# First layer of a two-layer block: half of the second GroupNorm's sums as running arrays instead of Gram products

## The reference

```
x = x + linear_attention(group_norm(x))     # layer 0
x = x + gated_conv(group_norm(x))           # layer 1
```

## Time and profile before

| what | value |
|---|---|
| three runs | 6730.23, 6728.38, 6723.05 us |
| median | 6728.38 us |
| the profiled execution's own time | 6717.27 us |
| its span | 6715.5 us |
| mean granted TensorE clock, share of full speed | 0.96 |
| busy over the span: PE, PEld, DVE, ACT, POOL | 85%, 78%, 67%, 54%, 61% |

### The profile page before, as it was taken

One profiled execution on the slowest core, in us unless ns is written; L12 is line 12 of the kernel. 1 busy time (PEld: TensorE's weight loads), 2 busy tenths in 40 slices (PEclk: granted clock), 3 DMA queues, 4 the chain that ended last, 5 costly groups with the idle time before them and its releaser, 6 DMA issues. The chain is left out here.

```text
span 6715.5 us, 144257 instructions
## 1 busy us (share of the span) xinstructions
PE 5725.9 (85%) x51796; PEld 5234.1 (78%) x51796; DVE 4511.4 (67%) x5284; ACT 3640.0 (54%) x4872; POOL 4125.6 (61%) x3608
## 2 busy tenths in 40 slices
PE   5789999999999999999984368888888888888887
PEld 5678888888888888888874368777877878777787
DVE  6367777777777777777763786666666666666653
ACT  5555555555555555555540445555555555555554
POOL 0146666666666666666667677676676767676751
PEclk8899999999999999999997789999999999999999
DMA  5356676666766667666656469899999999999987
GB/s 130 123 157 205 205 216 202 206 198 207 212 209 199 200 206 211 207 198 207 190 168 184 122 176 262 252 261 249 259 261 253 265 255 262 245 256 251 258 247 212
DMA packets 1239334, 1441.35 MB, mean 215 GB/s; under 512 B 142960, under 2 KB 1025396, under 8 KB 1238516
## 3 DMA queue, kind: packets, MB, share of 16 engines
q1 hardware_dynamic: 1238516, 1431.07, 75.0%
HBM read 999.09 MB, written 431.64 MB: 213 GB/s over the span
## 5 line engine op out<-in xcount | busy, mean ns | idle before, releaser
L1257 PE MATMUL psC<-wide,xhl 128*128 128x256 bf16 x6144 | 1037.1, 279 | 37.1 <-DVE xhl L1455 15.2
L1187 POOL TENSOR_TENSOR stage<-stage,nrow 128x1024 f32<-128x1024 f32 x240 | 620.0, 2583 | 407.8 <-DMA stage<-x_by_block_row 397.0
L1254 PE MATMUL psC<-wide,xhl 128*128 128x192 bf16 x6144 | 863.3, 250 | 0.0
L1204 POOL COPY down<-xhl 48x448 f32<-48x448 f32 x512 | 533.2, 1041 | 520.9 <-PE psC L1263 421.9
L813 POOL TENSOR_TENSOR y<-y,grow 128x1024 f32<-128x1024 f32 x256 | 603.9, 2359 | 323.7 <-DVE y L657 323.7
L1455 DVE SCALAR_TENSOR_TENSOR xhl<-xhl,psC 128x512 f32<-128x512 f32 x512 | 348.8, 682 | 503.7 <-ACT xhl L1348 503.0
L824 POOL TENSOR_TENSOR q<-q,qinv 128x1024 f32<-128x1024 f32 x256 | 490.0, 1914 | 308.6 <-DVE qinv L731 308.6
L1263 PE MATMUL psC<-narrow,down 128*128 128x96 bf16 x6144 | 527.3, 210 | 171.5 <-DMA narrow<-toeplitz_narrow 98.1
L657 DVE TENSOR_TENSOR y<-psProj,rstd 128x1024 f32<-128x1024 f32 x256 | 313.5, 1225 | 516.0 <-POOL rstd L805 516.0
L1348 ACT ACTIVATE xhl<-psC 128x512 f32<-128x512 f32 x512 | 304.3, 599 | 636.7 <-PE psC L1263 635.1
L1254 PEld LDWEIGHTS psC<-wide,xhl 128*128 128x128 bf16 x6144 | 639.3, 115 | 12.2
(11 more groups left out here) (181 smaller groups left out, 14276.2 us busy)
## 6 DMA issues: line engine op xcount, KB each, us to landing
wide<-toeplitz_wide SPq DMA_DIRECT2D x1024, 140.0 KB, 4.5
xa<-in_x SPq DMA_DIRECT2D x256, 512.0 KB, 4.7
xb<-in_x SPq DMA_DIRECT2D x256, 512.0 KB, 3.8
xc<-in_x SPq DMA_DIRECT2D x256, 512.0 KB, 5.7
x_rows<-xc SPq DMA_DIRECT2D x256, 512.0 KB
res<-x_rows SPq DMA_DIRECT2D x256, 512.0 KB, 7.2
out<-res SPq DMA_DIRECT2D x256, 512.0 KB, 6.4
stage<-x_by_block_row SPq DMA_DIRECT2D x225, 512.0 KB, 7.2
```

The source lines that it names most:

```text
L1187: nc.gpsimd.tensor_tensor(v, v, nrow[:, 0:1, :].to_broadcast([P, NP_, C]), ALU.mult).then_inc(s_scaled, 1)
L1204: nc.gpsimd.tensor_copy(dst[lo, :, :, 0:last], src[lo, :, 0:NQ, CW:])
L1254: nc.tensor.matmul(dst[:, :, :, 2:], lhs, tab[:, :, 32 + part * 12:44 + part * 12], start=False, stop=False)
L1257: nc.tensor.matmul(dst, lhs, tab[:, :, part * 16:part * 16 + 16], start=(n == 0), stop=False)
```

## The change

The chunk's 8 rows are parted. The Gram product takes rows 0 to 3 (TG = 4), so 8 passes of TensorE where there were 16. The other four rows (TS = 4), a [128, 4, 128] slice, go this way: GpSimd adds them to `acc1` at the end of the step in which it made x1; ScalarE squares them into `sq` at the beginning of the next step, ahead of qT; VectorE adds `sq` to `acc2` right behind y. At n = 2 of the next image TensorE's `turn_sums`, behind the projection, multiplies the four rows of `acc1` and of `acc2` by a column of ones and so adds over the partitions: into column 128 of psG and into a column of its own. `take_gram` moves from behind y to the end of VectorE's step, waits for that, and has one addition more. SyncE waits for the square and the running sum too before it reloads xc.

```diff
--- before.py
+++ after.py
@@ -255,6 +255,8 @@
     CHUNKS = IMGS * NCH
     W1 = C + 1
     BK = 96
+    TG = 4
+    TS = TPC - TG
     STORES = [16 * n for n in (4, 7, 4, 7)]
     with ExitStack() as ctx:
         sb = lambda n, s, d=F32: ctx.enter_context(nc.sbuf_tensor(n, s, d))
@@ -308,6 +310,9 @@
         norm_old = sb("norm_old", [P, 2])
         gram = sb("gram", [P, C])
         gsum = sb("gsum", [P, 2])
+        sq = sb("x1_squared", [P, TS, C])
+        acc1 = sb("x1_sum", [P, TS, C])
+        acc2 = sb("x1_square_sum", [P, TS, C])
         psR = [ps(f"psR{k}", [P, CT]) for k in range(2)]
         psO = ps("psProj", [P, CT])
         psC = ps("psCtx", [P, 512])
@@ -363,6 +368,11 @@
         g_done = sem("b_gram")
         s_gram = sem("b_gram_masked")
         g_taken = sem("b_gram_taken")
+        s_sq = sem("b_squared")
+        s_acc1 = sem("b_sum_added")
+        s_acc2 = sem("b_square_added")
+        s_fin = sem("b_sums_turned")
+        s_accgo = sem("b_sum_begun")
         block = ctx.enter_context(nc.Block())
         NCONST = 5
 
@@ -414,6 +424,8 @@
                         if not isinstance(img, int) or gc + 1 >= 4:
                             sp.wait_ge(s_store[k], img * (STORES[k] * NCH // 4) + (n + 1) // 4 * STORES[k])
                         sp.wait_ge(g_done, upto(gc - 2))
+                        sp.wait_ge(s_acc1, upto(gc - 2))
+                        sp.wait_ge(s_sq, upto(gc - 2))
                         sp.dma_start(xc[k][:, :, 0:C], x_chunk(img + (n + 1) // NCH, (n + 1) % NCH)
                                      ).then_inc(s_xc[k], 16)
                     if live(img, gc - 2):
@@ -465,10 +477,20 @@
                 if m == 0:
                     pe.wait_ge(g_taken, img)
                 v = xc[m % 4]
-                for t in range(TPC):
+                for t in range(TG):
                     mm = nc.tensor.matmul(psG[:, 0:W1], v[:, t, 0:C], v[:, t, :],
-                                          start=(m == 0 and t == 0), stop=(m == NCH - 1 and t == TPC - 1))
+                                          start=(m == 0 and t == 0), stop=False)
                 mm.then_inc(g_done, 1)
+
+            def turn_sums(img):
+                pe.wait_ge(s_acc1, img * NCH)
+                pe.wait_ge(s_acc2, img * NCH)
+                one = xc[0][:, 0, C:W1]
+                for t in range(TS):
+                    nc.tensor.matmul(psG[:, C:W1], acc1[:, t, :], one, start=False, stop=(t == TS - 1))
+                for t in range(TS):
+                    mm = nc.tensor.matmul(psG[:, W1:W1 + 1], acc2[:, t, :], one, start=(t == 0), stop=(t == TS - 1))
+                mm.then_inc(s_fin, 1)
 
             def turn_ek(n, ga, gb):
                 pe.wait_ge(k_exped, gb)
@@ -574,6 +596,8 @@
                         nc.tensor.transpose(psC[:, 128:256], accn[:], ident[:]).then_inc(s_m, 1)
                     if live(img, gc - 1):
                         project(img, n, gc)
+                    if n == 2 and image_live(img - 1):
+                        turn_sums(img)
                     if n == 0 and image_live(img):
                         pe.wait_ge(s_m, img * 7 + 4)
                         nc.tensor.matmul(psC[:, 256:384], wqkv[:, 2 * C:3 * C], ctxg[:], start=True, stop=True
@@ -588,6 +612,10 @@
             def image(img, steps):
                 for n in range(steps):
                     ga, gb, gc = indices(img, n)
+                    if live(img, gc - 3):
+                        act.wait_ge(s_x1, gc - 2)
+                        act.wait_ge(s_acc2, upto(gc - 3))
+                        nc.scalar.activation(sq[:], xc[(n - 3) % 4][:, TG:, 0:C], ACT.Square).then_inc(s_sq, 1)
                     if live(img, gb - 2):
                         act.wait_ge(qt_ready, gb - 1)
                         act.wait_ge(o_ready, upto(gc - 1))
@@ -740,13 +768,25 @@
                 mx = qmax[:, n % 2, :].unsqueeze(2).to_broadcast([P, TPC * HEADS, DH])
                 nc.vector.tensor_tensor(qv, v, mx, ALU.subtract).then_inc(q_subbed, 1)
 
+            def add_squares(img, n, gc):
+                dve.wait_ge(s_sq, gc - 2)
+                if (n - 3) % NCH == 0:
+                    if image_live(img - 1):
+                        dve.wait_ge(s_fin, img)
+                    nc.vector.tensor_copy(acc2[:], sq[:]).then_inc(s_acc2, 1)
+                else:
+                    dve.wait_ge(s_acc2, gc - 3)
+                    nc.vector.tensor_tensor(acc2[:], acc2[:], sq[:], ALU.add).then_inc(s_acc2, 1)
+
             def take_gram(img, gc):
-                dve.wait_ge(g_done, gc - 2)
+                dve.wait_ge(s_fin, img)
                 nc.vector.tensor_copy(gsum[:, 0:1], psG[:, C:W1])
                 nc.vector.tensor_tensor(gram[:], psG[:, 0:C], ident[:], ALU.mult).then_inc(s_gram, 1)
-                dve.wait_ge(s_gram, img * 2 - 1)
+                dve.wait_ge(s_gram, img * 3 - 2)
                 nc.vector.tensor_reduce(gsum[:, 1:2], gram[:], AX.X, ALU.add).then_inc(s_gram, 1)
-                dve.wait_ge(s_gram, img * 2)
+                dve.wait_ge(s_gram, img * 3 - 1)
+                nc.vector.tensor_tensor(gsum[:, 1:2], gsum[:, 1:2], psG[:, W1:W1 + 1], ALU.add).then_inc(s_gram, 1)
+                dve.wait_ge(s_gram, img * 3)
                 at = slice(img - 1, img) if isinstance(img, int) else bass.ds(img - 1, 1)
                 nc.vector.tensor_copy(sums2[:, :, at].squeeze(2), gsum[:]).then_inc(g_taken, 1)
 
@@ -768,8 +808,8 @@
                         dve.wait_ge(s_m, img * 7 + 7)
                         dve.wait_ge(o_ready, img * NCH)
                         nc.vector.tensor_tensor(M[:], psC[:, 384:512], brow[:], ALU.add).then_inc(s_mready, 1)
-                    if n == 2 and image_live(img - 1):
-                        take_gram(img, gc)
+                    if live(img, gc - 3):
+                        add_squares(img, n, gc)
                     if n == 0 and image_live(img + 1):
                         norm_weights(img, gb)
                     if n == 0 and live(img, gb - 1):
@@ -785,6 +825,8 @@
                             add_up(n, gb)
                     if live(img, gb):
                         centre_q(n, gb)
+                    if n == 2 and image_live(img - 1):
+                        take_gram(img, gc)
 
             all_images(dve, image)
 
@@ -822,6 +864,18 @@
                         qv = q[k][:].rearrange("p t (h d) -> p (t h) d", d=DH)
                         iv = qinv[:, k, :].unsqueeze(2).to_broadcast([P, TPC * HEADS, DH])
                         nc.gpsimd.tensor_tensor(qv, qv, iv, ALU.mult).then_inc(s_qn, 1)
+                    if live(img, gc - 2):
+                        v = xc[(n - 2) % 4][:, TG:, 0:C]
+                        pool.wait_ge(s_x1, gc - 1)
+                        if (n - 2) % NCH == 0:
+                            if image_live(img - 1):
+                                pool.wait_ge(s_fin, img)
+                            if not isinstance(img, int):
+                                pool.sem_inc(s_accgo, 1)
+                            nc.gpsimd.tensor_copy(acc1[:], v).then_inc(s_acc1, 1)
+                        else:
+                            pool.wait_ge(s_acc1, upto(gc - 2))
+                            nc.gpsimd.tensor_tensor(acc1[:], acc1[:], v, ALU.add).then_inc(s_acc1, 1)
 
             all_images(pool, image)
```

## The result

| what | before | after |
|---|---|---|
| median of four runs each | 6729.31 us | 6788.15 us |
| lowest and highest run | 6723.05, 6737.33 | 6767.97, 6791.86 |
| ratio after/before | | 1.0081, 95% from 1.0058 to 1.0103 |
| the profiled execution's own time, its span | 6717.27, 6715.5 | 6767.97, 6764.5 |
| end of layer 0 in it | 3659.51 | 3697.09 |

The change costs 59 us. The forecast said +70 (6798, range 6742 to 6865). Of the 49 us between the two profiled spans 37.6 arise in layer 0 and 11.4 behind it.

A forecast was written before the change was run, and what follows sets the result against it. The bound was a closed two-step loop through the Gram product, 12.19 us a step. Full images 44, last but one 3, last 21, tail 1: together 69 on 6728, rounded 6798 us; range 6742 to 6865.

The forecast's parts named there:

- two-step loop through the Gram product: Closed loop across engines in full steps, today's bound: 24.42 us over two steps, falling to 23.91, 11.96 a step.
- ScalarE loop: One-step loop from projection through ScalarE's work and `keys` to the next projection: 11.80 us, plus 0.50 for the square, 12.30.
- port loop: One-step loop from y through centring and row sums to the next y: 11.94 us, plus 0.38, 12.32.
- The lock's delay: VectorE's addition behind y holds back GpSimd's multiplication by g: 0.54 less some 0.16 of overlapping start-up, taken as 0.38 us.
- full-block rival: GpSimd's multiplication by g delayed by all of 0.54: port loop 12.48, 28 us more, 6826; chance 0.18.
- n = 1 to 4 [...] +0.9 net, the weakest figure: Steps n = 1 to 4 of each full image: gains and losses net +0.9 us, bounds -1 to +3.
- the step n = 0 [...] +0.85: Step n = 0 of each full image: 0.6 for the addition before the statistics, VectorE ending some 0.25 later; +0.85 us, an estimate.
- The last image: GpSimd is the bound there: running sum 1.1 and lock 0.38 add 1.5 us on each of 14 steps, 21 us.
- the clock should not answer: TensorE's granted clock stays despite the halved Gram: in the prologue it is busy 8.80 of 10.82 us and granted 1.00.
- Lock lost: GpSimd takes the port before the addition every step: 13.9 us a step, +1.7 on 165 steps, about 7030; chance 0.06.
- Loops shorter than added up: The square fits in ScalarE's slack, leaving 11.96 a full step: -38 us on 165 steps, total 6712; chance 0.14.
- TensorE the bound: TensorE bounds full steps and all 0.89 us of the halved Gram come back: -147 + 22, 6603; chance 0.02.

The follow-up runs named there:

- experiment 2: Kernel before with the Gram product halved to rows 0 to 3, sums of the other four rows left out: 6674.65 us, ratio 0.9928.
- experiment 4: Changed kernel with VectorE's addition of squares cut to 4 elements a partition: full step 12.39 us, step of the last image but one 11.75; no total given.
- experiment 1: Changed kernel with ScalarE's square moved from ahead of qT to behind it: 6733.34 us against 6724.92 for the kernel before, ratio 1.0007.
- experiment 3: Changed kernel with ScalarE's square cut to 4 elements a partition, in its old place ahead of qT: full step 12.12 us; no total given.
- experiment 6: Kernel before with one VectorE memset of 128x1 added behind y in every step: 6705.42 us, ratio 0.9974.
- experiment 5: Kernel before with only `take_gram` moved to the end of VectorE's step n = 2: 6717.83 us, ratio 0.9994.
- experiment 7: Kernel before with three tiles and five semaphores allocated and never used: 6718.65 us, ratio 0.9999.
- the repetition: Changed kernel and kernel before profiled once more, unedited, on one chip: spans 6763.9 and 6731.7 us, layer 0 ending at 3696.74 and 3657.46.
- before_again: Kernel before run once more, unedited, for a second profile: span 6731.7 us, layer 0 ending at 3657.46, 3074.2 behind it.

## Why the prediction was right, and where it was not

**The three loops.** Right. The two-step loop through the Gram product was the bound, the ScalarE loop and the port loop lay close under it, and both were made longer than it had been. Sizes:

| loop | forecast, before and after | measured |
|---|---|---|
| ScalarE | 11.80, 12.30 | 11.87 (experiment 2), 12.39 (after, experiment 4) |
| port | 11.94, 12.32 | 11.75 (experiments 2, 4), 12.12 (experiments 1, 3) |

The square was 0.52 for 0.50; between qT's end and `keys` there are 0.12 for the 0.05 that the earlier trace rows gave. The lock's delay was 0.37 for 0.38, though it shows as a longer L855, not as a later one. The port loop's base was 0.19 too long, for I took its hops from a step that it doesn't bind: in experiment 4 centring to row sums is 1.14 where I put 1.24, and y to centring 7.35 where the earlier trace rows give 7.44, since L818 starts 2.44 behind the multiplication and not 2.53. It does no harm, since ScalarE binds, but "within 0.02 of each other" was not so.

"SBUF — State Buffer" of the Trainium skill, section "Who interferes with whom", has the loser blocked for the winner's whole instruction. The row agrees on who blocks whom. VectorE's addition ends at 2017.80 + 0.68 = 2018.48 and L855, begun at 2017.96, takes 0.37 more than its 2.36, less than the 0.52 between its start and the addition's end. The hidden start-up that I allowed for is thus in the runs, and the full-block rival, 12.48, is refuted: the loop is 12.12.

**The turn of an image.** This is the wrong step: "n = 1 to 4 [...] +0.9 net, the weakest figure" and "the step n = 0 [...] +0.85", +1.75 together. Measured are -2.0 in the loop (+0.18 an image, of which 11 full steps are +2.2). Of it -2.4 is one piece, the turn with the loop's jump, in which VectorE stood still for 3 us before and no longer does. The earlier trace rows hold no row of that stall, and I never asked what ended the row sums' wait at n = 0; in the waits view it stands as an "issue" of 3.4 us. What the change does to it is no effect of what its instructions compute: a useless instruction takes it away too (experiment 6), a moved one (5) and unused tiles (7) don't. That instruction alone gives 1.7 of the 2.4; the other 0.7 was not parted, and the granted clock, 0.79 to 0.93 in the turns of before and 0.84 to 1.00 in those of after, is mixed into it. Outside the hardware loop, where neither engine stalls, the turns cost nothing much (20.24 and 20.03 before, 20.38 and 20.60 after) and an image costs +2.8 where 3.2 was said; in the repetition it was +3.9, with those two turns at 21.87 and 21.37 and a clock of 0.84 for 0.92. So 14 images gave about 8 us instead of 44. `turn_sums` takes 1.8 of TensorE for the 2.0 said (two groups of 0.97 less what they overlap), and n = 2 to 3 pays only 0.69 of it: moving `take_gram` late gives 1.2 back there by itself (experiment 5), as the earlier trace rows's locked copy goes.

Of the cause of the stall the runs show what it goes with. In the six traces of kernels whose VectorE program has its old number of instructions a step it is there at 11 turns; in the eight of kernels with one more (the memset or the addition of squares) it is at none. Fewer fetch packets go with that, 381 in the six and 333 or 286 in the eight. That the engine waits for its own instructions behind the jump is my reading. "Runtime: NRT & Kernel Launch" of the Trainium skill, section "Instruction fetch mechanics", says that a taken branch to a target outside the two pages that an engine holds costs a fetch before it can go on; the trace agrees in what it shows, 3 us of VectorE and 2.6 of TensorE with no wait named, at the jump alone. No run here moves the target by known amounts, so this stays open.

**The last image.** Forecast +21, measured +27.1 (26.1 in the repetition). The steps were right: 15 of them went from a mean of 7.98 to 9.44, 22.0, with 1.18 for the running sum where 1.1 was said and 0.37 for the lock. What I missed is one step, n = 2 to 3, 12.60 where it was 7.82: +4.8; my 21 held nothing for `turn_sums` and the late `take_gram` there. The timeline of after shows why:

```profile
3542.81 1.71 PE L490 MATMUL psGram<-xc,x_sum 128*128 128x1 f32 x8
3543.06 1.02 ACT L644 ACTIVATE sqo<-psProj 128x1024 f32<-128x1024 f32 x1 [7.67 <-PE psProj L550]
...
3544.38 1.85 PE L492 MATMUL psGram<-xc,x_square_sum 128*128 128x1 f32 x8
...
3546.26 0.16 DVE L783 COPY gsum<-psGram 128x1 f32<-128x1 f32 x1 [6.54 <-PE psGram L492]
...
3547.24 1.22 DVE L679 TENSOR_REDUCE vsum<-sqo 128x8 f32<-128x1024 f32 x1
```

`turn_sums` takes 3.4 at half the clock (granted 0.50, 1.2 GHz instead of 2.4), `take_gram` waits for it, and the row sums, whose input is ready at 3543.06 + 1.02 = 3544.08, stand behind it until 3547.24. In the repetition `turn_sums` ran at the full clock here, 1.8, and the step took 11.00. So 1.6 of the 4.8 is the clock and 3.2 is that the row sums have to wait for `turn_sums` and `take_gram` at all. Some 0.3 is left for the rest. I had written "the clock should not answer", on the earlier trace rows's prologue, which has full clock with little TensorE work; it did answer, 0.86 to 0.59. In the other 15 steps that costs nothing, since GpSimd's loop is as long.

**What is unexplained.** The medians say +59, with 39 to 69 as the interval; the traces of both pairs say +38 and +39 for layer 0. The part behind layer 0 is word for word alike in all kernels, and over the 14 traces it takes 3049 to 3087. In the six traces with the running arrays it takes 3067 to 3087, mean 3074; in the eight without, 3049 to 3074, mean 3059. A single trace, `before_again`, makes the two groups overlap, so most of the other 21 us of the medians seems to arise there. Experiment 1 says the same: its layer 0 ends 6 to 8 us earlier than that of the kernel before, at 3651.45, and its time is 8 us longer, if anything. Why untouched code should be slower behind the change no run shows; unused tiles and semaphores do not do it (3049, experiment 7).

**The rivals.** Lock lost: VectorE gets in first in 224 of the 240 additions traced. It loses at n = 1 of each image, where the product for M stands between y and the addition, which then lasts 2.87 (15 times); step n = 1 to 2 is longer by only 0.09. What costs little once an image was not a case for every step. Loops shorter than added up: refuted for ScalarE, half true for the port. (The page of before has a second activation of that size, L1363, 0.60 and from PSUM as well; the square, from SBUF, is recorded at 0.64 and costs 0.52.) TensorE the bound: refuted by experiment 2, 11.87 for 11.30. The total was close partly by luck: the terms were 31 too high against the trace (36 too much for the turns, 6 too little for the last image), and the medians differ by 21 more than layer 0 does.

## What to carry to other kernels

Before you take work off the busiest engine, look for closed loops across engines, two steps long ones too: here the same 0.9 us could be freed by moving half of the product one place in its own queue (ratio 0.989), where handing it to three other engines cost 0.8%. An instruction put into an engine's gap-free stretch cost 0.52 of its 0.64 us here, and one place further on, nothing. Read "issue" waits at the turns of hardware loops before pricing an edit: an edit of that engine's program may remove them, and a useless instruction is the cheap test of it.

## What the runs showed of the hardware

- A hardware loop's jump can hold VectorE for 3.0 us (row sums 6.06 behind the projection instead of 3.05), at each of 11 jumps, and one 128 x 1 write more in the program takes it away. TensorE is held 2.6 us at the same jumps, with and without that write.
- Taking away half of one product, with all else alike, dropped TensorE's granted clock from 0.86 to 0.60 in a stretch in which it waits a lot, and made a projection there 3.76 us long instead of 2.02 to 2.6: less work made the last image 22 us longer (143.7 to 165.7).
- In eleven turns of one kernel, the same work took 19.8 to 20.0 us where TensorE was granted its full clock and 21.8 to 23.0 where it was granted 0.85 to 0.92 of it.
- Locked out at its start, a 128x1024 GpSimd multiplication took 2.73 us instead of 2.36: it is recorded as running while it waits, so the lock hides in the duration, not in the gap ahead of it.
